# A Mamba and mixture-of-experts layer in one kernel: the four z products in one slot as raw copies, their silu in one group, and three other moves

## The chip, the cores and the metric

The kernel runs on one core of one Trainium2 chip. Its time is the device time of one execution in microseconds; below, "us" is always that. The time of a version is the median of several executions.

## What is computed

Two sequences of 4096 tokens with 256 features go through a layer of two residual branches:

```python
x = x + layernorm(mamba(layernorm(x)))
x = x + layernorm(ffn(layernorm(x)))

# mamba: W_in gives x_in and z (512 channels each)
xz = einsum('bld,de->ble', x, W_in)
x_in, z = split(xz, 2)
u = silu(causal_conv4(x_in) + conv_b)            # 4 taps per channel
dt_lr, Bm, Cm = split(u @ W_xproj)               # 16, 16, 16
delta = softplus(dt_lr @ W_dt + b_dt)
h = exp(delta * A) * h + (delta * u) * B_t       # 16 states per channel, over 4096 steps
y = (sum over states of h * C_t) + D_skip * u
out = (y * silu(z)) @ W_out

# ffn: a shared expert, and the two best of 8 experts by a softmax router
shared = (silu(x @ shared_gate) * (x @ shared_up)) @ shared_down
routed = sum over e of coef[t, e] * ((silu(x @ gate_e) * (x @ up_e)) @ down_e)
```

## The kernel before

**Tiling.** The 8192 tokens are cut into 16 chunks of 512 (`CHUNKS`). The 512 channels are 4 groups of 128 partitions (`J`), the tokens of a chunk 4 blocks of 128 (`NT`). A chunk's scan has 16 states times 4 channel groups: 64 slots (`SLOTS`), one scan instruction (L753, VectorE) in each. Slot t handles state t // 4, group t % 4.

**Stages.** Every engine runs the same loop, `body(s, lo, r)`, for s = -2 to 17. In body s the scan is that of chunk s (`with_scan`), the out-projection, norms and FFN are those of chunk s-1 (`ffn`), and the x and z products, convolution, silu and softplus are those of chunk s+1 (`prep`). The norm of the input of chunk s+2 (tile `xa`) is made too. So bodies 2 to 14 all hold the same work; body 0 has no FFN part, and body 15 no prep part. Body -1 is the prologue, body 16 the FFN of the last chunk with no scans.

**Order of the work.** Each engine's instructions are written out by hand: a table of slot numbers (`XIN_PE`, `SILU`, `Y_POOL` and so on, from L188) says in which of the 64 slots an engine issues a step, and the order of the `if`s in `body` sets the order inside a slot. Engines meet only by semaphores (a `Stage` holds one, `at(chunk, k)` is the count to wait for).

**What happens between slot 60 of one body and slot 14 of the next,** where the change lies:

- ScalarE makes `d_a` (the decay, exp, L602) two slots ahead of the scan: the one for scan t+2 is issued in slot t and waits until scan t has freed one of the two PSUM banks. So the scans and ScalarE are coupled: whatever ScalarE does between two decays must fit beside the VectorE work of the same slots. exp and silu use different function tables; the compiler puts an ACT_TABLE_LOAD before the first of each run. Copies and Identity are issued under either.
- TensorE transposes the states (L445) so that VectorE can add them into `y_t` (L763, two adds in every even slot; state 0 is copied by ScalarE, L610, slots 5 to 8). It also makes the x products (L433, slots 4, 4, 7, 8), which ScalarE and VectorE turn into the convolution `u` (L698, then L907, slots 6, 7, 10, 11), and the z products (L556): groups 0 and 1 in slot 9 into the banks `dn`, groups 2 and 3 in slots 60 and 61 into the banks `ring`. ScalarE takes silu of u 0, 1 and z 0, 1 in slot 8, of u 2, 3 in slot 11, and of z 2, 3 in slot 62.
- The transposes of the normed input (`x_t`, L423) are in slot 0 of body s for chunk s+1, and their copies (L688) in slot 1.
- The out-projection: `y_d` (L770) in slot 3, times silu(z) on GpSimd (`gate_y`, L1033, slot 4, behind that slot's `d_bu`), the products with W_out (L469, slots 5 and 6), then the norm's moments on VectorE (`O_STATS`, slot 8: L774, L780), its rstd on GpSimd (`rstd_of("o")`, L953 to L961), the add to the stream (L786, slot 9), the moments and rstd of x1, the normed x1 (ScalarE, L619), its transposes (TensorE, L490, slot 10) and copies (ScalarE, L660).
- GpSimd makes the inflow `d_bu` (L987) in every even slot, keeps the last column of each state (L1026, every fourth slot), multiplies the FFN's hidden tiles (L1040, L1045), makes the six small operations of the convolution's head (`before_chunk`, L932 to L944) in slot 1, and adds the FFN's result to the stream (`add_stream_y`, L976) in slot 7.
- The moments of the FFN's result (`Y_STATS`, slot 60) stand in VectorE's order between scan 60 and the two adds of slot 60. They wait for the last down products (L536).

## Time and profile before

| | |
|---|---|
| median of 3 runs | 2431.92 us (2430.57 to 2432.0) |
| the profiled execution | 2430.07 us |
| its span, first to last instruction | 2428.1 us |
| granted TensorE clock, mean | 0.938 |
| busiest engine | VectorE, 2228.7 us, 92% of the span |
| VectorE waits for others, whole span | 171 us, of which 47.4 in one wait of the last body |

The profiled execution took 1.85 us less than the median. The span is 1.97 us shorter than that execution's own time. A row of a timeline has the start in us, the duration (for "x2" of the merged pair), engine, line, operation, tiles and shapes; the bracket is how long the engine was idle before it, and what released it. A row of a window has each engine's busy time in that stretch and the clock granted to TensorE (1.00 is 2.4 GHz, 0.50 is 1.2 GHz).

### The profile page before, as it was taken

To read this page: it belongs to the slowest core of one execution; us is meant where nothing else is said; L and a number is where in the kernel's file an instruction comes from. 1 tells how busy PE (TensorE), PEld (TensorE's weight loads), DVE (VectorE), ACT (ScalarE), POOL (GpSimd) and SP (SyncE) were. 2 spreads that over 40 slices of the span, in tenths; PEclk is the share of its full clock that TensorE was granted. 3 is DMA by queue.
4 is the path that set the end of the run, shared out by engine and by line. 5 is a ranking of instruction groups with operands and counts; after the bars stand their busy time and mean duration, and the time that the engine had idled before them with its cause. 6 is when DMAs were issued, how large, how long until landed. Compare 5 with 4: busy or idle time off the path is not lost. (4 is left out here: it accounts for less than half of the span.)

```text
span 2428.1 us, 29696 instructions
## 1 busy us (share of the span) xinstructions
PE 2073.8 (85%) x8960; PEld 1322.8 (54%) x8960; DVE 2228.7 (92%) x3176; ACT 1601.1 (66%) x2358; POOL 1906.6 (79%) x1566
## 2 busy tenths in 40 slices
PE   5668989889898988989888898888989898896977
PEld 2445555656555555655655555555555555564544
DVE  3999999999999999999999999999999999998950
ACT  4556767676776767777677676667677676675632
POOL 3576887969789696978969788796978879698844
PEclk9659999999999999999999899999999999998989
DMA  4111211111121121111211121121112111111101
GB/s 135 34 34 42 70 53 57 58 49 57 53 62 57 49 57 58 57 53 58 65 46 47 58 65 55 55 57 50 56 53 62 61 49 53 49 57 48 65 23 44
DMA packets 92943, 134.23 MB, mean 55 GB/s; under 512 B 12000, under 2 KB 42976, under 8 KB 92784
## 3 DMA queue, kind: packets, MB, share of 16 engines
q1 hardware_dynamic: 92784, 132.34, 18.2%
q8 instruction: 72, 1.18, 0.2%
q14 instruction: 87, 0.71, 0.1%
HBM read 123.13 MB, written 9.18 MB: 54 GB/s over the span
## 5 line engine op out<-in xcount | busy, mean ns | idle before, releaser
L753 DVE TENSOR_TENSOR_SCAN h<-d_a,carry,d_bu 128x512 f32<-128x512 f32 x1024 | 1262.0, 1267 | 35.8 <-ACT d_a L602 35.4
L987 POOL TENSOR_TENSOR d_bu<-delta_u,b_rows 128x1024 f32<-128x1024 f32 x512 | 1202.3, 2357 | 5.1 <-DMA b_rows<-b_rows_hbm 0.9
L602 ACT ACTIVATE d_a<-delta,a_neg 128x512 f32<-128x512 f32 x1024 | 696.4, 689 | 622.2 <-DVE h L753 620.2
L445 PE MATMUL ht<-ident,h 128*128 128x128 f32 x4096 | 618.1, 295 | 116.8 <-DVE y_t L763 111.8
L445 PEld LDWEIGHTS ht<-ident,h 128*128 128x128 f32 x4096 | 503.7, 151 | 367.5 <-issue 132.0
L763 DVE SCALAR_TENSOR_TENSOR y_t<-ht,c_t,y_t 128x512 f32<-128x512 f32 x960 | 665.5, 734 | 2.8 <-PE ht L445 2.6
L509 PE MATMUL ring<-x_t,w_gate_sb 128*128 128x512 f32 x640 | 329.1, 641 | 20.6 <-ACT delta L718 19.1
L516 PE MATMUL ring<-x_t,w_up_sb 128*128 128x512 f32 x640 | 296.4, 606 | 23.0 <-ACT silu_gate L671 22.8
L536 PE MATMUL dn<-w_down_sb,hidden 128*128 128x256 f32 x1280 | 304.3, 381 | 13.2 <-POOL hidden L1045 13.2
L1040 POOL TENSOR_TENSOR hidden<-silu_gate,up 128x512 f32<-128x512 f32 x160 | 204.3, 1277 | 135.8 <-ACT up L675 77.9
L536 PEld LDWEIGHTS dn<-w_down_sb,hidden 128*128 128x128 f32 x1280 | 236.0, 190 | 74.8 <-issue 31.8
L1026 POOL TENSOR_TENSOR carry<-h,one 128x4 f32<-128x4 f32 x256 | 51.2, 200 | 238.7 <-DVE h L753 238.4
L516 PEld LDWEIGHTS ring<-x_t,w_up_sb 128*128 128x128 f32 x640 | 116.6, 191 | 151.7 <-issue 117.0
L602 ACT ACT_TABLE_LOAD x152 | 195.0, 1283 | 2.7
L509 PEld LDWEIGHTS ring<-x_t,w_gate_sb 128*128 128x128 f32 x640 | 121.3, 210 | 121.8 <-issue 90.7
L1045 POOL TENSOR_TENSOR hidden<-hidden,coef_rows 128x512 f32<-128x512 f32 x128 | 162.6, 1271 | 10.0
L907 DVE SCALAR_TENSOR_TENSOR u<-ring,conv_w_sb,u 128x511 f32<-128x511 f32 (+2 forms) x192 | 143.7, 748 | 6.8
L433 PE MATMUL ring<-x_t,w_in_sb 128*128 128x512 f32 x256 | 124.0, 629 | 17.7 <-DVE y_d L770 10.8
L469 PE MATMUL dn<-w_out_sb,y_d 128*128 128x256 f32 x512 | 114.5, 382 | 7.1 <-POOL y_d L1033 7.1
L774 DVE BATCH_NORM_STATS2 stats_o<-dn 128x6 f32<-128x256 f32 x128 | 45.4, 416 | 74.1 <-PE dn L536 65.4
L469 PEld LDWEIGHTS dn<-w_out_sb,y_d 128*128 128x128 f32 x512 | 96.0, 190 | 22.6 <-POOL y_d L1033 10.2
L675 ACT ACTIVATE up<-ring 128x512 f32<-128x512 f32 x160 | 92.8, 580 | 22.4 <-PE ring L516 22.4
(111 smaller groups left out, 1868.7 us busy)
## 6 DMA issues: line engine op xcount, KB each, us to landing
b_rows<-b_rows_hbm SPq DMA_DIRECT2D x256, 256.0 KB, 3.5
coef_rows<-coef_rows_hbm SPq DMA_DIRECT2D x128, 256.0 KB, 3.5
xa<-L_attn_x_in SPq DMA_DIRECT2D x16, 512.0 KB, 5.1
xr<-L_attn_x_in SPq DMA_DIRECT2D x16, 512.0 KB, 5.2
out<-xr SPq DMA_DIRECT2D x16, 512.0 KB, 2.9
w_in_sb<-L_attn_W_in_in SPq DMA_DIRECT2D x1, 1024.0 KB, 6.4
w_gate_sb<-L_ffn_experts_gate_in SPq DMA_DIRECT2D x2, 512.0 KB, 4.5
w_up_sb<-L_ffn_experts_up_in SPq DMA_DIRECT2D x2, 512.0 KB, 5.4
```

The source lines that it names most:

```text
L445: last = nc.tensor.transpose(HT[q % HTS][:, j * P:(j + 1) * P], H[:, (NS * c + n) % HS, j, a * P:(a + 1) * P], IDN[:, :])
L469: last = nc.tensor.matmul(DN[a // 2][:, (a % 2) * DM:(a % 2 + 1) * DM], YD[:, j, a * P:(a + 1) * P], WO[:, j, :], start=(j == 0 and a % 2 ...
L509: last = nc.tensor.matmul(bank[:, :], WG[:, k, f, :], X1T[:, k, :], start=(k == 0), stop=(k == KM - 1))
L516: last = nc.tensor.matmul(bank[:, :], WU[:, k, f, :], X1T[:, k, :], start=(k == 0), stop=(k == KM - 1))
L536: last = nc.tensor.matmul(DN[a // 2][:, (a % 2) * DM:(a % 2 + 1) * DM], HF[:, f % 2, a * P:(a + 1) * P], WD[:, f, :], start=(f == 0 and a ...
L602: nc.scalar.activation(DA[i % DAS][:, :], DL[:, r, j, :], ACT.Exp, scale=ANEG[:, j, n:n + 1]).then_inc(ex.sem, 1)
L753: nc.vector.tensor_tensor_scan(H[:, (NS * s + n) % HS, j, :], DA[(n * J + j) % DAS][:, :], BU[:, (2 * n + j // 2) % 4, j % 2, :], CARRY[:, ...
L763: nc.vector.scalar_tensor_tensor(YT[:, a, :], HT[q % HTS][:, :], CT[:, r, a, n:n + 1], YT[:, a, :], ALU.mult, ALU.add).then_inc(add_c.sem, 1)
L907: nc.vector.scalar_tensor_tensor(U[:, o, j, back:], bank[:, 0:T - back], CW[:, j, k:k + 1], U[:, o, j, back:], ALU.mult, ALU.add)\
L987: nc.gpsimd.tensor_tensor(BU[:, (2 * n + h) % 4, :, :], DU[:, 2 * h:2 * h + 2, :], BB[:, n % 2, :].unsqueeze(1).to_broadcast([P, 2, T]), A ...
L1040: nc.gpsimd.tensor_tensor(HF[:, f % 2, :], TG[:, f % 2, :], UP[:, f % 2, :], ALU.mult).then_inc(hf.sem, 1)
L1045: nc.gpsimd.tensor_tensor(HF[:, f % 2, :], HF[:, f % 2, :], CB[:, e % 2, :], ALU.mult)\
```

## The change

Five things move; all numbers are slots.

1. **z products.** All four (L555 in the new file) are in slot 9, through the two banks `dn` in turn. ScalarE copies each raw into `silu_z` (L713; groups 0 and 1 in its slot 8, 2 and 3 in its slot 9 behind the normed x1), counted by the new semaphore `z_raw`. TensorE waits for copy j-2 before product j, and for all four before it transposes x1 into the same banks. The silu of all four (L719), in place, is one group in slot 60. In the prologue (no chunk to scan) it stands behind the silu of u 2, 3 in slot 11 (`SILU_FIRST`).
2. **x_t.** The transposes of chunk s+2 go to slot 58 of body s, the copies to slot 59, instead of slots 0 and 1 of the next body. The moments of `xa` are spread over slots 26, 32, 36 and 42, closed in slot 46, with the rstd in 47 and the normed `xa` in 50.
3. **Tap groups' silu.** The silu of u 0 and 1 is in slot 7, ahead of state 0's copy of that slot.
4. **GpSimd.** The head of the convolution is in slot 15 of the body before. `gate_y` stands ahead of `d_bu` in slot 4. `add_stream_y` is in slot 8, behind `rstd_of("o")`.
5. **Y_STATS** is still in slot 60, behind that slot's two adds.

```diff
-        Y_POOL = 7
+        Y_POOL = 8
-        XA_STATS, XA_RSTD, XA_NORM = (32, 32, 42, 42), 44, 49
+        XA_STATS, XA_MEAN, XA_RSTD, XA_NORM, XT_PE, XT_ACT = (26, 32, 36, 42), 46, 47, 50, 58, 59
-        Z_PE, Y_STATS = (9, 9, 60, 61), 60
-        SILU = {8: [("u", 0), ("u", 1), ("z", 0), ("z", 1)], 11: [("u", 2), ("u", 3)], 62: [("z", 2), ("z", 3)]}
+        Z_PE, Z_ACT, Y_STATS = 9, (8, 8, 9, 9), 60
+        U_EARLY, HEAD_POOL = 7, 15
+        SILU = {11: [("u", 2), ("u", 3)], 60: [("z", j) for j in range(J)]}
+        SILU_FIRST = {11: SILU[11] + SILU[60]}
...
                 if t == X1T_PE:
                     if exists(lo + 1):
-                        pe.wait_ge(sz.sem, sz.at(s + 1, 2))
+                        pe.wait_ge(z_raw.sem, z_raw.at(s + 1))
...
                         if j < 2:
                             pe.wait_ge(resid["o"].sem, resid["o"].at(s - 1, 2 * j + 2))
                         else:
-                            pe.wait_ge(*ring_user_before(s, lo, "z", j))
+                            pe.wait_ge(z_raw.sem, z_raw.at(c, j - 1))
                         for k in range(KM):
-                            last = nc.tensor.matmul(z_bank(j)[:, :], WIN[:, k, DI + j * P:DI + (j + 1) * P],
+                            last = nc.tensor.matmul(DN[j % 2][:, :], WIN[:, k, DI + j * P:DI + (j + 1) * P],
...
+                    if prep and t == U_EARLY:
+                        for k in range(2):
+                            silu_u(s + 1, o, k)
                     if with_scan and NT < t <= 2 * NT:
                         first_state(s, r, t - NT - 1)
...
+                for j in range(J):
+                    if t == Z_ACT[j]:
+                        act.wait_ge(full["z"].sem, full["z"].at(c, j + 1))
+                        act.wait_ge(y_gate.sem, y_gate.at(s - 1))
+                        nc.scalar.activation(SZ[:, o, j, :], DN[j % 2][:, :], ACT.Copy).then_inc(z_raw.sem, 1)
...
+                        nc.scalar.activation(SZ[:, o, k, :], SZ[:, o, k, :], ACT.Silu).then_inc(sz.sem, 1)
...
-                    if with_scan and n + 1 < NS and t % 2 == 0:
-                        inflow(s, n + 1, t % NT // 2)
-                    if ffn and t == 60:
-                        rstd_of("y", s - 1)
                     if ffn and t == Y_GATE:
                         for j in range(J):
                             gate_y(s - 1, o, j)
+                    if with_scan and n + 1 < NS and t % 2 == 0:
+                        inflow(s, n + 1, t % NT // 2)
...
-                    if prep and t == 1:
-                        before_chunk(s + 1, o)
+                    if exists(lo + 2) and t == HEAD_POOL:
+                        before_chunk(s + 2, r)
```

**ScalarE, slots 7 to 11 of a body with all parts.** Before (L610 is state 0's copy, L694 and L698 the taps of an x product, L704 silu of u, L708 silu of z, L619 the normed x1, L660 the copies of its transposes):

```order
271 L610 ACTIVATE y_t<-ht,c_t 128x512
272 L694 ACTIVATE halo<-ring 128x3
273 L698 ACTIVATE u<-ring,conv_b_sb,conv_w_sb 128x509
274 L694 ACTIVATE halo<-ring 128x3
275 L698 ACTIVATE u<-ring,conv_b_sb,conv_w_sb 128x509
276 L704 ACT_TABLE_LOAD
277 L704 ACTIVATE u<-u 128x512 x2
278 L708 ACTIVATE silu_z<-dn 128x512 x2
279 L602 ACT_TABLE_LOAD
280 L602 ACTIVATE d_a<-delta,a_neg 128x512
281 L619 ACTIVATE up<-xr,mean_rstd_x,rstd_x 128x256 x4
283 L660 ACTIVATE x_t<-dn 128x512 x2
```

And with the change, from the silu of u 0 and 1 on (L694 is now the silu of u, L713 the raw copies, L618 the normed x1, L668 the copies of its transposes):

```order
272 L694 ACT_TABLE_LOAD
273 L694 ACTIVATE u<-u 128x512 x2
274 L609 ACTIVATE y_t<-ht,c_t 128x512
275 L601 ACT_TABLE_LOAD
279 L706 ACTIVATE u<-ring,conv_b_sb,conv_w_sb 128x509
281 L706 ACTIVATE u<-ring,conv_b_sb,conv_w_sb 128x509
282 L713 ACTIVATE silu_z<-dn 128x512 x2
283 L601 ACTIVATE d_a<-delta,a_neg 128x512
284 L618 ACTIVATE up<-xr,mean_rstd_x,rstd_x 128x256 x4
285 L713 ACTIVATE silu_z<-dn 128x512 x2
286 L601 ACTIVATE d_a<-delta,a_neg 128x512
287 L668 ACTIVATE x_t<-dn 128x512 x2
```

The silu group of slot 8 has lost its two z and moved ahead of the taps; two copies stand before the normed x1, and two between it and the copies of its transposes.

**GpSimd, slots 0 to 9 of such a body.** Before:

```order
245 L987 TENSOR_TENSOR d_bu<-delta_u,b_rows 128x1024
246 L932 TENSOR_TENSOR head<-halo,conv_w_sb 128x12
251 L944 TENSOR_TENSOR head<-head,conv_b_sb 128x12
254 L987 TENSOR_TENSOR d_bu<-delta_u,b_rows 128x1024
255 L1033 TENSOR_TENSOR y_d<-y_d,silu_z 128x512 x4
256 L987 TENSOR_TENSOR d_bu<-delta_u,b_rows 128x1024
257 L976 TENSOR_TENSOR xr<-xr,silu_gate 128x1024
258 L1026 TENSOR_TENSOR carry<-h,one 128x4
259 L987 TENSOR_TENSOR d_bu<-delta_u,b_rows 128x1024
260 L953 TENSOR_TENSOR var_eps_o<-mean_var_o,eps 128x4
```

With the change:

```order
243 L998 TENSOR_TENSOR d_bu<-delta_u,b_rows 128x1024 x2
244 L1037 TENSOR_TENSOR carry<-h,one 128x4
245 L1044 TENSOR_TENSOR y_d<-y_d,silu_z 128x512 x4
246 L998 TENSOR_TENSOR d_bu<-delta_u,b_rows 128x1024 x2
247 L1037 TENSOR_TENSOR carry<-h,one 128x4
248 L998 TENSOR_TENSOR d_bu<-delta_u,b_rows 128x1024
249 L964 TENSOR_TENSOR var_eps_o<-mean_var_o,eps 128x4
251 L972 TENSOR_TENSOR mean_rstd_o<-mean_var_o,rstd_o 128x4
252 L987 TENSOR_TENSOR xr<-xr,silu_gate 128x1024
253 L964 TENSOR_TENSOR var_eps_x<-mean_var_x,eps 128x4
```

The head is gone from slot 1, `gate_y` passed one `d_bu`, and `add_stream_y` (the xr row) passed from before `rstd_o` to behind it.

**ScalarE, slots 58 to 63.** Before, the silu of z 2, 3 stands between the decays 0 and 1 of the next chunk, and the copies of x_t behind the next body's decay 3:

```order
251 L602 ACTIVATE d_a<-delta,a_neg 128x512 x7
252 L708 ACT_TABLE_LOAD
253 L708 ACTIVATE silu_z<-ring 128x512 x2
254 L602 ACT_TABLE_LOAD
255 L602 ACTIVATE d_a<-delta,a_neg 128x512 x2
256 L628 ACTIVATE silu_gate<-dn,mean_rstd_y,rstd_y 128x256 x4
257 L602 ACTIVATE d_a<-delta,a_neg 128x512
258 L688 ACTIVATE x_t<-ring 128x512 x2
```

With the change the copies stand before decay 62 and the group of four before decay 63:

```order
254 L601 ACTIVATE d_a<-delta,a_neg 128x512 x4
255 L657 ACTIVATE x_t<-ring 128x512 x2
256 L601 ACTIVATE d_a<-delta,a_neg 128x512
257 L719 ACT_TABLE_LOAD
258 L719 ACTIVATE silu_z<-silu_z 128x512 x4
259 L601 ACT_TABLE_LOAD
260 L601 ACTIVATE d_a<-delta,a_neg 128x512 x4
```

The number of table loads in such a body is the same; the group is two silu longer and two slots earlier.

## Rows read from the trace of the kernel before

**Rows 1.** The page, busy time, share of the span and instructions of each engine

```profile
PE 2073.8 (85%) x8960; PEld 1322.8 (54%) x8960; DVE 2228.7 (92%) x3176; ACT 1601.1 (66%) x2358; POOL 1906.6 (79%) x1566
```

**Rows 2.** The waits of VectorE: us in total, times, longest

```profile
DVE stats_o L774 <- PE dn L536: 65.4, 16, 47.4
DVE h L753 <- ACT d_a L602: 35.4, 78, 12.4
DVE xr L786 <- POOL rstd_o L956: 21.4, 16, 2.5
```

**Rows 3.** The timeline of VectorE, slot 60 to slot 14 of the next body

```profile
746.57 1.42 DVE L774 BATCH_NORM_STATS2 stats_o<-dn 128x6 f32<-128x256 f32 x4 [1.20 <-PE dn L536]
748.33 1.38 DVE L763 SCALAR_TENSOR_TENSOR y_t<-ht,c_t,y_t 128x512 f32<-128x512 f32 x2
...
780.86 1.66 DVE L786 SCALAR_TENSOR_TENSOR xr<-dn,rstd_o,xr 128x256 f32<-128x256 f32 x4 [1.28 <-POOL rstd_o L956]
...
796.86 1.28 DVE L753 TENSOR_TENSOR_SCAN h<-d_a,carry,d_bu 128x512 f32<-128x512 f32 x1 [0.32 <-ACT d_a L602]
```

**Rows 4.** The timeline of GpSimd, slots 1 to 16 of that body

```profile
761.32 0.21 POOL L932 TENSOR_TENSOR head<-halo,conv_w_sb 128x12 f32<-128x12 f32 x1
...
774.69 2.35 POOL L976 TENSOR_TENSOR xr<-xr,silu_gate 128x1024 f32<-128x1024 f32 x1
...
777.16 2.35 POOL L987 TENSOR_TENSOR d_bu<-delta_u,b_rows 128x1024 f32<-128x1024 f32 x1
...
779.74 1.02 POOL L956 TENSOR_TENSOR rstd_o<-var_eps_o,minus_half 128x4 f32<-128x4 f32 x1
...
784.32 0.20 POOL L953 TENSOR_TENSOR var_eps_x<-mean_var_x,eps 128x4 f32<-128x4 f32 x1 [3.28 <-DVE mean_var_x L780]
...
800.71 0.20 POOL L1026 TENSOR_TENSOR carry<-h,one 128x4 f32<-128x4 f32 x1 [5.42 <-DVE h L753]
```

**Rows 5.** The timeline of VectorE, slot 9 of body 1

```profile
204.94 1.66 DVE L786 SCALAR_TENSOR_TENSOR xr<-dn,rstd_o,xr 128x256 f32<-128x256 f32 x4 [0.30 <-POOL rstd_o L956]
```

**Rows 6.** The timeline of TensorE, slots 9 and 10, and slot 59

```profile
744.54 1.99 PE L536 MATMUL dn<-w_down_sb,hidden 128*128 128x256 f32 x8 [0.82 <-POOL hidden L1045]
...
781.79 3.70 PE L556 MATMUL dn<-x_t,w_in_sb 128*128 128x512 f32 x8 [0.66 <-DVE xr L786]
788.79 2.07 PE L490 MATMUL dn<-ident,up 128*128 128x128 f32 x8 [3.31 <-ACT up L619]
```

**Rows 7.** The timeline of ScalarE, slots 9 to 13

```profile
788.07 2.06 ACT L619 ACTIVATE up<-xr,mean_rstd_x,rstd_x 128x256 f32<-128x256 f32 x4
...
790.69 1.08 ACT L660 ACTIVATE x_t<-dn 128x512 f32<-128x512 f32 x2
...
794.83 1.28 ACT L602 ACT_TABLE_LOAD   x1
796.13 1.30 ACT L602 ACTIVATE d_a<-delta,a_neg 128x512 f32<-128x512 f32 x2
```

**Rows 8.** The timeline of GpSimd, slots 44 and 47

```profile
860.99 0.20 POOL L953 TENSOR_TENSOR var_eps_xa<-mean_var_xa,eps 128x4 f32<-128x4 f32 x1
...
865.93 1.28 POOL L1040 TENSOR_TENSOR hidden<-silu_gate,up 128x512 f32<-128x512 f32 x1 [0.80 <-issue]
```

**Rows 9.** The timeline of VectorE, the first scan of body 0

```profile
50.51 1.28 DVE L753 TENSOR_TENSOR_SCAN h<-d_a,carry,d_bu 128x512 f32<-128x512 f32 x1 [12.43 <-ACT d_a L602]
```

**Rows 10.** The timeline of VectorE, slots 8 and 9 of body 15

```profile
2212.18 1.62 DVE L774 BATCH_NORM_STATS2 stats_o<-dn 128x6 f32<-128x256 f32 x4 [2.05 <-PE dn L469]
...
2217.89 1.66 DVE L786 SCALAR_TENSOR_TENSOR xr<-dn,rstd_o,xr 128x256 f32<-128x256 f32 x4 [2.51 <-POOL rstd_o L956]
```

**Rows 11.** Windows: busy us of PE, PEld, DVE, ACT, POOL, then clock, DMA share, GB/s

```profile
140.00:160.00 20.00, 11.98 (x50) 10.05 (x51) 19.97 (x28) 10.57 (x18) 13.46 (x12) 0.50 0.14 39
```

**Rows 12.** The timeline of TensorE, x products 0 and 1 of bodies 0 and 9

```profile
57.98 6.66 PE L433 MATMUL ring<-x_t,w_in_sb 128*128 128x512 f32 x8 [4.38 <-ACT x_t L688]
...
1339.32 4.28 PE L433 MATMUL ring<-x_t,w_in_sb 128*128 128x512 f32 x8
```

57 lines of the change are left out of this document (29 added, 28 removed).

## The prediction

> **What bounds the kernel now.** I read the page first: VectorE is busy for 2228.7 of 2428.1 us [rows 1], so in the steady bodies only VectorE's waits can be won, and 199 us of idle is all there is. Then the waits of VectorE [rows 2]. The 65.4 us on the down products hold one of 47.4 in the last body; the other 15 are 1.20 each. The 21.4 us before L786 are 13 of about 1.3, and three more at both ends. Of the 35.4 us on decays, 17.9 lie in body 0; the rest is about 1.1 per body in pieces. Then the timeline of VectorE over one seam between bodies [rows 3], which I follow slot by slot: from slot 60 to slot 14 it stands still three times, 1.20 us before the moments of y, 1.28 before L786, 0.32 before scan 14. Last, the other engines in the same stretch [rows 4, 6, 7], to see what each wait ends on and what is late next. The order of VectorE hardly changes, so this is a change of what VectorE waits for.
>
> **Moments of y behind the two adds.** The down products end at about 746.5 [rows 6], the moments start at 746.57, 1.20 after scan 60. The two adds take 1.38, less what overlaps the next instruction, 1.30 [rows 3], so they fill the 1.20. Not all of it stays. The rstd of xa (four small operations, 1.8 us of GpSimd from 860.99) moves from slot 44, where GpSimd had 0.80 idle behind it, to slot 47, ahead of the hidden tile of 865.93 [rows 8]. With the moments of xa closed in slot 46 (by the replay of VectorE's scans at about 864.5) it ends at 866.4, so that tile is 0.45 later; 0.15 of that is absorbed on the way, and the down products of slot 59, which wait for GpSimd already [rows 6], come 0.3 later. The moments then wait 0.3 instead of 1.20. The closing of xa's moments in slot 46 fills a 0.2 wait for a decay. **Gain 1.0 per body**, between 0.2 (if the rest of GpSimd's queue passes on more of its 1.8) and 1.4.
>
> **GpSimd before rstd_o.** In slot 8 the moments of o are ready about 1 us before GpSimd comes to them at 779.5, when `d_bu` (2.35 us from 777.16) ends; ahead of that stood `add_stream_y` (2.35 from 774.69) and the six head operations (0.21 each and gaps, 1.34 in all from 761.32) [rows 4]. With both gone from before it (3.7 us, of which the later rstd of xa takes 0.3), GpSimd is free at about 776.2. What the wait is then, body 1 shows, which has no `add_stream_y` yet: 0.30 [rows 5]. **Gain 0.98 per body.** `add_stream_y` behind rstd_o hides beside L786 and the x1 moments: 2.35 against the 3.28 that GpSimd stood idle there. `gate_y` ahead of one `d_bu` makes that `d_bu` ready at 771.4; scan 8, wants it at about 774. The head in slot 15 lies in 5.42 us of idle [rows 4]. All three cost nothing; without that cover each would cost its own length.
>
> **z products in slot 9, the chain to scan 14.** This takes back. Counting from the start of L786 (780.86), before: the first product at 0.93, the second ready at 4.67 [rows 6], silu 0.6, table load 1.28, decay 11 0.69 (two take 1.30), the four normed x1 from 7.2 to 9.2, their transposes behind them from 7.9, the copies from 9.8, decay 13, load, two silu, load, and decay 14 ends at 16.0, which is when scan 14 starts [rows 3, 7]. Now: TensorE runs four products, 7.4 us, from 1.0 to 8.3. ScalarE copies z 0 at 3.0 and z 1 at 4.7, decay 11 follows at 5.3 with no load, the normed x1 run from 5.95 to 7.95, the copies of z 2 and 3 to 9.1. The transposes start at 9.2, and as all four x1 are there, they take about half of the paced 2.07, 1.04. Copies 10.1 to 11.1, decay 13, load 1.28, two silu 1.15, load 1.28, decay 14 at 16.25. VectorE without waits needs 15.7. So scan 14 waits 0.55 instead of 0.32: **cost 0.25 per body**. The bounds: VectorE-bound, a gain of 0.32, and a cost of 2.1 if nothing of the transposes' pacing is won back and the copies queue one behind the other. I take the replay, since each duration in it is a row. The product of slot 9 that sets it off also waits for TensorE itself: x products, states and out-projection in front of it end at 779.7, L786's second result at 779.6. TensorE has next to no slack there.
>
> **ScalarE, slots 58 to 63.** The copies of x_t (1.06 us) and the group of four silu (load 1.28, 2.3, load 1.28) put decay 63 at about 752.0; scan 63 wants it at 752.2. Nothing lost, with 0.2 to 0.3 of cover, which is there because the moments of y stand in slot 60. In body 0 there are none: **1.9 us lost once**. Here a rule is weighed. The row shows a load of 1.28 us and the next activation 1.30 after its start, at 794.83 and 796.13 [rows 7]. The Trainium skill (ScalarE: Activation LUTs, What ACT_TABLE_LOAD costs) gives 1283 ns for the load and another 1380 ns of drain for every switch; by that, decay 63 would be 2.8 later and some 35 us would be lost over the bodies. The load agrees, of the drain the trace shows nothing.
>
> **Silu of u 0, 1 in slot 7** starts when convolution 1 is done, at 774.3, and leaves ScalarE before the x products 2, 3 need it; no VectorE wait hangs on it, between 0 and 0.2 of cost.
>
> **The ends.** Body 15 has no z and no convolution. There L774 waits 2.05 for the out-projection and L786 2.51 for rstd_o [rows 10]; `gate_y` one `d_bu` (2.35) earlier and GpSimd free give back 1.1 and 2.2; with the 1.0 of body 14's moments 4.3, and 1.2 for its own. The prologue pays. Scan 0 waits 12.43 on ScalarE [rows 9]. There z 2, 3 and all four silu now come before `x_dbl` (about 4.2 us), and the copies of x_t, with a wait for TensorE, before decay 0 (2). Against that, the silu group between decays 0 and 1 is gone (3.65), and scans 1 to 6 wait no more: 2.6 late at the first convolution, and 1.7 more by slot 14 of body 0, where no FFN work covers four products: 4.3 in all, between 0 and 7.
>
> **The sum.** Per body 1.0 + 0.98 - 0.25 = 1.73, for the 13 seams before bodies 2 to 14: 22.5. Body 15 4.3 + 1.2. Against: prologue and body 0 4.3, its slot 60 1.9, body 1 0.1. That is 28.0 - 6.3 = 21.7. I take off 2 for the clock, see below: 19.7. The profiled execution took 2430.07, so 2410.4; the median of the runs lies 1.85 above it, so I forecast **2412 us**.
>
> **The rivals.**
> 1. *The low clock reaches the x products.* In body 0, with little but transposes, TensorE is granted 0.50, its lower level of 1.2 GHz [rows 11]. At each seam only transposes now run from the down products to the x products, 16 us instead of 12. Before, 3 of 14 seams entered the x products at the low clock and lost 0.6 (4.28 against 3.67 [rows 12]); that is where my 2 us come from. If half of each group runs low, TensorE is 1 us later at z 0, and so is decay 14: 13 us lost, 2425. The Trainium skill (TensorE: Matmul & The Clock Gate, the entries on transpose mode) says that transposes don't count as activity as matmuls do; body 0's 0.50 agrees.
> 2. *The z chain makes it slower.* The same place, at full price: a whole group at the low clock takes 6.66 instead of 3.67 [rows 12], 3 us later at z 0 with no slack, and 13 times 3 is 39 against the 21.7: 2449. It turns slower from 1.7 us per seam on. For it: no slack on TensorE and one more handshake (TensorE, ScalarE, TensorE) per bank. Against: in the trace the clock came back within the first products, whenever it had fallen.
> 3. *No loss at scan 14.* If the two engines overlap better than I replayed, scan 14 waits for nothing: 0.57 more per body, 7 us: 2403.
> 4. *Nothing is won:* the chain to decay 14 keeps its old end, since every gain before it only lengthens the wait there. Then only body 15's 5.5 is left, against 6.3: 2432.
> 5. *The drain of the skill's rule* shows where the cover is thin: a loss at decay 63 of 2.5 us in 14 bodies, 2445.
>
> **How the numbers follow.** Forecast (2405 to 2419) 0.57; rival 1 0.16; rival 2 0.07; rival 3 0.11; rival 4 0.08; rival 5 0.01. Range 2401 to 2427: it takes in rivals 1 and 3, the bounds of the prologue, and 0.4 us per body to either side. A measurement of this kernel can tell 0.2%, 4.9 us, from no change. Faster 0.85, same 0.07, slower 0.08.
>
> **What would show it.** The wait of the y moments at 0.3 (right) or near 1.2; that before L786 at 0.3; the wait before scan 14 at 0.5 to 0.6, not 2; scan 63 without a wait but in body 0; scan 0 at about 57. Wrong would be: a VectorE wait at scan 14 of over 1.5, x products of over 5 us at most seams, or new waits before scans 2 and 4.

## The result, and the profile after the change

| | before | with the change |
|---|---|---|
| median | 2431.24 us (2429.9 to 2432.0, 4 runs) | 2404.24 us (2401.76 to 2408.07, 4 runs) |
| profiled execution, its span | 2430.07, 2428.1 | 2401.76, 2400.0 |
| granted clock, mean | 0.938 | 0.922 |

The ratio is 0.9891, with a 95% interval of 0.9874 to 0.9908: 1.1% faster. The forecast was 2412, within 2401 to 2427. The profiled execution is the fastest of the four, 2.5 us under their median, so a sum of waits read from its trace and a difference of medians can differ by some us.

In the new file the scan is L764, the decay L601, the adds into `y_t` L774, the moments L785 and L791, the add to the stream L797, the down products L537, the x products L434, the raw z copies L713. The waits of VectorE (us in total, times, longest), which answer to [rows 2]:

```profile
DVE stats_o L785 <- PE dn L537: 52.9, 14, 47.4
DVE h L764 <- ACT d_a L601: 37.2, 43, 17.8
...
DVE xr L797 <- POOL rstd_o L967: 7.9, 16, 1.8
```

Beside the 47.4 of the last body, 5.5 us in 13 waits are left for the down products (18 before), and 7.9 for rstd_o (21.4 before). The decays cost slightly more in total, in 43 waits instead of 78: one of 17.8 is scan 0. Busy time has hardly changed, VectorE's least of all (compare [rows 1]):

```profile
PE 2065.5 (86%) x8960; PEld 1344.7 (56%) x8960; DVE 2225.6 (93%) x3176; ACT 1628.4 (68%) x2420; POOL 1907.1 (79%) x1566
```

The timeline of VectorE over the same seam as [rows 3]:

```profile
744.57 1.42 DVE L785 BATCH_NORM_STATS2 stats_o<-dn 128x6 f32<-128x256 f32 x4 [0.41 <-PE dn L537]
...
776.55 1.66 DVE L797 SCALAR_TENSOR_TENSOR xr<-dn,rstd_o,xr 128x256 f32<-128x256 f32 x4 [0.30 <-POOL rstd_o L967]
...
792.59 1.28 DVE L764 TENSOR_TENSOR_SCAN h<-d_a,carry,d_bu 128x512 f32<-128x512 f32 x1 [0.37 <-ACT d_a L601]
```

The start of L797 (L786 before) is a good mark for timing a body, since it comes once in each. Between bodies 1 and 14 its starts lie 1871.35 us apart before (204.94 to 2076.29) and 1842.05 after (209.39 to 2051.44): 143.95 and 141.70 per seam. I call the mean per seam **the distance** below. The span lost 28.1 us: the 13 seams won 29.3, bodies 14 and 15 won 3.6 more, 4.45 are given back up to body 1, and 0.3 in the epilogue.

Ten of the 13 seams look like the one above. Three have a long wait at scan 14, as here:

```profile
509.98 1.28 DVE L764 TENSOR_TENSOR_SCAN h<-d_a,carry,d_bu 128x512 f32<-128x512 f32 x1 [1.53 <-ACT d_a L601]
```

The timeline of TensorE in that seam shows why. The transposes of `y_t` take 1.97 and 1.91 (1.09 and 1.04 where the clock is back in time), and the x products behind them 4.89 instead of 3.67. From 475.57 on TensorE never stops, so the z products start at 494.97, 2.2 us after L797 instead of 0.9:

```profile
473.81 1.97 PE L459 MATMUL ring<-ident,y_t 128*128 128x128 f32 x8 [1.18 <-DVE y_t L774]
475.57 1.91 PE L459 MATMUL dn<-ident,y_t 128*128 128x128 f32 x8
477.28 4.89 PE L434 MATMUL ring<-x_t,w_in_sb 128*128 128x512 f32 x8
...
494.97 7.03 PE L555 MATMUL dn<-x_t,w_in_sb 128*128 128x512 f32 x16
```

The other seams with slow x products are those whose L797 starts at 1059.59 (4.79, wait 1.43) and 1626.06 (4.87, wait 1.50); 4.00 goes with a wait of 0.63.

### The profile page after: what moved, and what is told of

Same layout as the page of the kernel before. It is cut to its first block and busy times, and to the rows that moved or that the text cites. A ratio compares the mean times of both kernels' runs of the same rounds, so it can differ in the third digit from the quotient of the medians.

```text
span 2400.0 us, 29790 instructions
## 1 busy us (share of the span) xinstructions
PE 2065.5 (86%) x8960; PEld 1344.7 (56%) x8960; DVE 2225.6 (93%) x3176; ACT 1628.4 (68%) x2420; POOL 1907.1 (79%) x1566
## 5 line engine op out<-in xcount | busy, mean ns | idle before, releaser
L764 DVE TENSOR_TENSOR_SCAN h<-d_a,carry,d_bu 128x512 f32<-128x512 f32 x1024 | 1262.0, 1267 | 40.5 <-ACT d_a L601 37.2
L601 ACT ACTIVATE d_a<-delta,a_neg 128x512 f32<-128x512 f32 x1024 | 696.4, 689 | 583.6 <-DVE h L764 581.8
L446 PEld LDWEIGHTS ht<-ident,h 128*128 128x128 f32 x4096 | 517.9, 154 | 376.3 <-DVE y_t L774 156.0
L774 DVE SCALAR_TENSOR_TENSOR y_t<-ht,c_t,y_t 128x512 f32<-128x512 f32 x960 | 665.6, 735 | 1.6 <-PE ht L446 1.2
L510 PE MATMUL ring<-x_t,w_gate_sb 128*128 128x512 f32 x640 | 314.8, 616 | 25.0 <-ACT delta L729 21.0
L537 PE MATMUL dn<-w_down_sb,hidden 128*128 128x256 f32 x1280 | 304.3, 381 | 15.5 <-POOL hidden L1056 15.5
L517 PE MATMUL ring<-x_t,w_up_sb 128*128 128x512 f32 x640 | 298.6, 610 | 21.7 <-ACT silu_gate L679 21.4
L537 PEld LDWEIGHTS dn<-w_down_sb,hidden 128*128 128x128 f32 x1280 | 235.9, 190 | 77.1 <-issue 28.7
L510 PEld LDWEIGHTS ring<-x_t,w_gate_sb 128*128 128x128 f32 x640 | 113.5, 197 | 122.7 <-issue 83.8
L434 PE MATMUL ring<-x_t,w_in_sb 128*128 128x512 f32 x256 | 128.2, 646 | 6.3 <-DVE y_d L781 3.4
L555 PE MATMUL dn<-x_t,w_in_sb 128*128 128x512 f32 x256 | 113.3, 595 | 0.7 <-DVE xr L797 0.7
```

Of the source, the lines that this page charges most:

```text
L446: last = nc.tensor.transpose(HT[q % HTS][:, j * P:(j + 1) * P], H[:, (NS * c + n) % HS, j, a * P:(a + 1) * P], IDN[:, :])
L510: last = nc.tensor.matmul(bank[:, :], WG[:, k, f, :], X1T[:, k, :], start=(k == 0), stop=(k == KM - 1))
L517: last = nc.tensor.matmul(bank[:, :], WU[:, k, f, :], X1T[:, k, :], start=(k == 0), stop=(k == KM - 1))
L537: last = nc.tensor.matmul(DN[a // 2][:, (a % 2) * DM:(a % 2 + 1) * DM], HF[:, f % 2, a * P:(a + 1) * P], WD[:, f, :], start=(f == 0 and a ...
L601: nc.scalar.activation(DA[i % DAS][:, :], DL[:, r, j, :], ACT.Exp, scale=ANEG[:, j, n:n + 1]).then_inc(ex.sem, 1)
L764: nc.vector.tensor_tensor_scan(H[:, (NS * s + n) % HS, j, :], DA[(n * J + j) % DAS][:, :], BU[:, (2 * n + j // 2) % 4, j % 2, :], CARRY[:, ...
```

## The experiments

All times below are medians, and "distance" is the mean over the same 13 seams of the profiled run. Each diff is against the changed kernel unless it says otherwise.

### Moments of y ahead of the adds again

In VectorE's order, the block goes back into `ffn_part`, which stands ahead of the adds:

```diff
+                if t == Y_STATS:
+                    dve.wait_ge(down.sem, down.at(c))
+                    for a in range(NT):
+                        moments("y", c, a, dn(a))
+                    moments_end("y", c)
...
-                    if ffn and t == Y_STATS:
-                        dve.wait_ge(down.sem, down.at(s - 1))
-                        for a in range(NT):
-                            moments("y", s - 1, a, dn(a))
-                        moments_end("y", s - 1)
```

> The changed kernel, with the moments of y put back between scan 60 and the two adds; all else stays. Theory (the prediction's first term): the adds no longer cover the end of the down products, so VectorE waits 0.4 + 1.3 = 1.7 us at L785 instead of 0.42 in the 14 bodies that have these moments, 16 to 18 us in all: 2418 to 2423. Rival: most of what the seams won came from elsewhere (GpSimd, the xa moments), and the wait comes back only at the size of 0.2 to 0.4 per body: 2407 to 2411.

2425.01 us, ratio to before 0.9974 (0.9965 to 0.9983). Distance 143.37.

```profile
750.73 1.43 DVE L785 BATCH_NORM_STATS2 stats_o<-dn 128x6 f32<-128x256 f32 x4 [1.74 <-PE dn L537]
```

The wait is 1.70 to 1.75 in all 13 bodies, as the theory had it. The distance is 1.67 longer, 1.3 of it from this wait; 0.4 to 0.5 in most bodies are waits for transposed states in the middle of the body. Against that, the x products take 3.60 wherever all eight are recorded from body 1 on, and no scan 14 waits over 0.37, which is 0.3 less per seam. So the first term holds at its full size. One line of position is worth 21 us; this wait alone makes 17 in the 13 seams. The time lies 2 us above the theory's range, which did not have the waits for transposed states.

### The moments of xa as before

```diff
-        XA_STATS, XA_MEAN, XA_RSTD, XA_NORM, XT_PE, XT_ACT = (26, 32, 36, 42), 46, 47, 50, 58, 59
+        XA_STATS, XA_MEAN, XA_RSTD, XA_NORM, XT_PE, XT_ACT = (32, 32, 42, 42), 42, 44, 49, 58, 59
```

> The changed kernel, with the moments, rstd and norm of xa in their old slots (32, 32, 42, 42, closed in 42; 44; 49). Theory: the spread moments fill waits of 0.19 for decays, which come back at three places per body (0.6 us), while rstd of xa no longer stands ahead of a hidden tile and the wait before the moments of y falls by about 0.2: net 0.3 to 0.4 in 14 bodies, 4 to 6 us slower, 2408 to 2410. Rival 1: only the later rstd counts, and the kernel is 2 to 4 us faster. Rival 2: nothing, within 1 us.

2405.44 us, ratio 0.9901 (0.9886 to 0.9916), distance 141.64. Rival 2 holds (1.2 us more, with intervals that overlap), and both mechanisms are there. Three waits of 0.19 for decays are back in each body, as before:

```profile
860.81 2.46 DVE L764 TENSOR_TENSOR_SCAN h<-d_a,carry,d_bu 128x512 f32<-128x512 f32 x2 [0.19 <-ACT d_a L601]
...
886.77 1.41 DVE L785 BATCH_NORM_STATS2 stats_o<-dn 128x6 f32<-128x256 f32 x4
```

And the moments of y wait for nothing any more. The first combined version below, where the closing and the rstd of xa go back and the spread stays, has no such wait either, so the whole 0.41 came from them. What comes back (0.57) is made good by this 0.41 and by the long waits at scan 14, which don't occur here (0.50 is the longest; 0.28 less per seam).

### GpSimd's two moves taken back

```diff
-        Y_POOL = 8
+        Y_POOL = 7
...
-                    if exists(lo + 2) and t == HEAD_POOL:
-                        before_chunk(s + 2, r)
+                    if prep and t == 1:
+                        before_chunk(s + 1, o)
```

> The changed kernel, with add_stream_y back in slot 7 and the head of the convolution back in slot 1; gate_y stays ahead of d_bu. Theory (the prediction's second term): rstd_o is late again, the wait before L797 goes from 0.30 to about 1.3 in bodies 2 to 14 and by 1 to 2 in body 15, so 13 to 16 us slower, 2417 to 2420, and the waits at scan 14 stay. Rival: L797 later means that the chain to scan 14 has its time in the wait either way, and half or less of it shows: 2404 to 2410.

2437.73 us, ratio 1.0034 (1.0022 to 1.0047): slower than the kernel before. Distance 144.12. Both sides were wrong: 33 us, twice the theory's figure.

```profile
788.12 1.66 DVE L797 SCALAR_TENSOR_TENSOR xr<-dn,rstd_o,xr 128x256 f32<-128x256 f32 x4 [2.64 <-POOL rstd_o L967]
```

The wait is 2.64, not 1.3. GpSimd's timeline in this run has one stop of 1.00 at 727.48, for the mean of xa, and none over 0.15 from there to rstd_o at 787.00:

```profile
727.48 0.20 POOL L964 TENSOR_TENSOR var_eps_xa<-mean_var_xa,eps 128x4 f32<-128x4 f32 x1 [1.00 <-DVE mean_var_xa L791]
...
781.93 2.38 POOL L987 TENSOR_TENSOR xr<-xr,silu_gate 128x1024 f32<-128x1024 f32 x1
...
787.00 1.02 POOL L967 TENSOR_TENSOR rstd_o<-var_eps_o,minus_half 128x4 f32<-128x4 f32 x1
```

That is 59.5 us in which GpSimd is the bound, and it explains the distance: L797 starts at 642.75, the chain begins 84.73 later, takes 59.52, and L797 follows rstd_o's start by 1.12, together 145.37 for this seam. It is one with a long wait at scan 14 (below); in most of the others the chain begins 83.03 after L797, and 83.03 + 59.52 + 1.12 = 143.67, as they are. Nothing that VectorE wins behind the mean of xa can shorten it; it only waits longer for rstd_o. The chain also begins later than before, when GpSimd had the rstd of xa behind it by slot 44 and stood idle for 0.80 ahead of the hidden tile [rows 8]. In waits, 1.36 more here stand against 0.78 fewer at the moments of y and 0.57 fewer at three decays. So with GpSimd as it was, all other parts together win nothing in a seam. Whether xa in its old slots would have left some of it wasn't tried.

In four bodies (2, 4, 8 and 14, three of them in the distance) scan 14 waits 2.06 instead of 0.36, 0.4 per seam, where the three long waits of the changed kernel made 0.3. There the x products are fast (3.67 at most), but TensorE stands idle for 2.34 to 2.68 before the z products, and these take 8.83 where all are recorded, instead of 7.13; in body 2 the granted clock is 0.85 and 0.72 in the windows from 352 to 360. In the other bodies from 3 on TensorE stands idle there for 1.62 to 2.21, and they take 7.13.

### GpSimd's three moves alone

Against the kernel before:

```diff
-        Y_POOL = 7
+        Y_POOL = 8
...
+                    if ffn and t == Y_GATE:
+                        for j in range(J):
+                            gate_y(s - 1, o, j)
                     if with_scan and n + 1 < NS and t % 2 == 0:
                         inflow(s, n + 1, t % NT // 2)
...
-                    if prep and t == 1:
-                        before_chunk(s + 1, o)
+                    if exists(lo + 2) and t == 15:
+                        before_chunk(s + 2, r)
```

> The kernel before with GpSimd's three moves alone (add_stream_y in slot 8, head in slot 15, gate_y ahead of d_bu). Theory: GpSimd runs without a stop from its last hidden tiles to rstd_o, so its moves and the gains ahead of rstd_o are two limits of one stretch: without GpSimd's moves the others won nothing there, and alone they win only their own wait, 1.28 to 0.30, in 13 seams, and 3 to 4 in body 15: 16 us, 2413 to 2417, with a distance between bodies of about 142.9. Rival: the wait before L786 was fed by all parts together, and GpSimd's moves alone win nearly the 33 us that taking them out cost: 2400 to 2405.

2419.43 us, ratio 0.9953 (0.994 to 0.9967), distance 143.31. The wait for rstd_o is 0.30 and that before the moments of y 1.20, as the theory says, and four seams take 142.75, 0.98 less than most had before; the other nine take 143.4 to 144.0, and in each of these VectorE waits 0.3 to 0.9 for transposed states (L445) in the middle of the body. The gain is 11.5 us, smaller than the 16 expected. Alone, GpSimd's moves win 0.64 per seam; two of them, taken out of the whole, cost 2.42 (the third, `gate_y`, is worth nothing in a seam, see below). The terms don't add, and this is the largest thing that the prediction's form, a sum of parts, did not see.

### z products as before

Against the kernel before: GpSimd's three moves as above, the moments of y behind the adds, and

```diff
-        XA_STATS, XA_RSTD, XA_NORM = (32, 32, 42, 42), 44, 49
+        XA_STATS, XA_MEAN, XA_RSTD, XA_NORM = (26, 32, 36, 42), 46, 47, 50
```

> The kernel before with all parts of the change but the z products, the copies of x_t and the place of the silu of u: z 0, 1 in slot 9 with silu in slot 8, z 2, 3 in slots 60 and 61 with silu in slot 62, x_t in slots 0 and 1; moments of y behind the adds, xa spread, GpSimd's three moves. Theory: the z move itself wins nothing. Its costs go: 4.5 of the prologue, 1.7 at scan 63 of body 0, and three waits of 1.1 at scan 14, while scan 14 waits 0.3 as before; so 6 to 10 us faster than the changed kernel, 2394 to 2398. Rival: the z move holds part of the gain, since copies of x_t and a silu group at the start of a body (between decays 0 and 1, behind decay 3) cost VectorE waits once the wait before the moments of y is gone: 2405 to 2415, with waits at scans 1 to 4 of each body.

2400.3 us, ratio 0.9875 (0.9861 to 0.9888), distance 141.84, L797's counterpart in body 1 at 204.57 instead of 209.39. So 4.8 us of the prologue come back, and the seams lose 0.14 each: scan 14 waits 0.24 to 0.48 everywhere, but two bodies have a wait of 1.84 and 2.04 before the moments of y. That is 2 us short of the theory's 2394 to 2398, and the rival's waits at scans 1 to 4 are not there. The intervals of this kernel and of the changed one overlap; it is 4 us ahead by the medians. The z move, which names the change, wins nothing measurable, and the combined versions below show that it costs.

### z products 2 and 3 beside the last hidden tiles

```diff
-        Z_PE, Z_ACT, Y_STATS = 9, (8, 8, 9, 9), 60
+        Z_PE, Z_ACT, Y_STATS = (9, 9, 55, 56), (8, 8, 57, 57), 60
...
-        RING_USE += [("xt", 2, k, k) for k in range(KM)]
+        RING_USE += [("z", 1, j, j % 2) for j in range(2, J)] + [("xt", 2, k, k) for k in range(KM)]
```

> The changed kernel, with z products 2 and 3 in slots 55 and 56 through the banks ring and their raw copies in slot 57; the silu of all four stays one group in slot 60. Theory: the four products in slot 9 cost the wait at scan 14 where the x products run at the low clock (1.4 to 1.5 in three bodies instead of 0.37); with two products TensorE has 3.6 us of room, so those three waits go, scan 14 waits 0.4 or less everywhere, and the prologue is 1.5 to 3.5 shorter, with scan 0 at about 53 to 54: 2397 to 2401. Rival: the two copies and two products beside the last FFN tiles delay the down products, and the wait before the moments of y grows by more than 0.5 per body: 2408 or more.

2426.7 us, ratio 0.998 (0.9971 to 0.9989), distance 143.19. Scan 14 indeed waits for nothing (under 0.15 in every body), also where the x products are slow (4.74 and 4.83 in bodies 11 and 13). So a long wait at scan 14 takes both, slow x products and four z products behind them. But the two products run back to back ahead of a transposed state, which is late for its add:

```profile
743.69 3.60 PE L558 MATMUL ring<-x_t,w_in_sb 128*128 128x512 f32 x8
747.12 1.04 PE L449 MATMUL ht<-ident,h 128*128 128x128 f32 x8
```
```profile
747.76 1.41 DVE L777 SCALAR_TENSOR_TENSOR y_t<-ht,c_t,y_t 128x512 f32<-128x512 f32 x2 [1.92 <-PE ht L449]
```

1.9 us in each of 14 bodies: the rival's size by another mechanism than it named. Scan 0 comes at 59.37, not 53 to 54. In this kernel the prologue's last copies of z and their silu stand in slot 57, ahead of decay 0.

### z of chunk 0 later in the prologue

```diff
-                    if t == Z_PE:
+                    if t == (Z_PE if exists(lo) else CT_PE + 1):
...
-                    if t == Z_ACT[j]:
+                    if t == (Z_ACT[j] if exists(lo) else XA_NORM + 1):
...
-        SILU_FIRST = {11: SILU[11] + SILU[60]}
+        SILU_FIRST = {11: SILU[11]}
+        Z_LATE = {7: (0, 1), 11: (2, 3)}
```

`Z_LATE` is the silu of chunk 0's z, in those slots of body 0.

> The changed kernel, with the z products of chunk 0 behind c_t in the prologue (slot 49), their raw copies in slot 51, and their silu in body 0 beside the silu of u (slots 7 and 11). Theory: x_dbl in the prologue waits for TensorE's four z products and four silu (from 34.0 to 42.8 on ScalarE), which all go from before it; scan 0 starts at 47 to 50 instead of 56.21, and all that follows is that much earlier, less 1 to 2 for the silu in body 0: 2396 to 2399. Rival: the chain to scan 0 runs over the input of chunk 1 (its norm, transposes and copies before decay 0), which doesn't move: scan 0 later than 53, 2401 or more.

2411.28 us, ratio 0.991 (0.9897 to 0.9924): 7 us above the changed kernel, with scan 0 at 60.56 instead of 56.21. `x_dbl` is copied 2.9 us earlier (39.88 instead of 42.79), and the delta is ready at 47.0. But ScalarE works in order, and the four copies now stand between the norm of xa and decay 0; they wait for TensorE until 56.95. The rival's side holds: the chain runs over what stands ahead of decay 0.

### Matmuls among the transposes

```diff
+        KEEP = (SLOTS - NT - 2, SLOTS - NT, SLOTS - NT + 2)
...
                 pe.wait_ge(*added(before, p))
+                if q in KEEP:
+                    nc.tensor.matmul(HT[q % HTS][:, :], WO[:, 0, 0:P], WIN[:, 0, 0:512], start=True, stop=True)
```

> The changed kernel with three matmuls of 128x512 added, of no use, one each before the transposes that stand in slots 59, 63 and 0, into the bank that these transposes then fill; nothing is left out. Theory: the clock falls because only transposes run from the down products to the x products; with matmuls among them it stays at 1.00 in the windows up to the x products, those take 3.67 or less in every body, no scan 14 waits over 0.7, and the kernel is 2 to 4 us faster than the changed one (2400 to 2402), unless the 0.9 us each makes a transposed state late for its add. Rival: three matmuls change nothing of the clock, and each is 0.9 to 1.8 us more on TensorE: waits of VectorE for transposes (L446), 2408 or more.

2426.16 us, ratio 0.9978 (0.9969 to 0.9987), distance 143.22. Each side is half right. The x products take 3.67 wherever all eight are recorded from body 1 on, and no scan 14 waits over 0.37 (windows: busy us of PE, PEld, DVE, ACT, POOL, then the clock):

```profile
751.00:752.00 1.00, 0.00 (x0) 0.00 (x0) 1.00 (x2) 0.98 (x2) 0.87 (x2) 0.82 0.18 66
752.00:753.00 1.00, 0.00 (x0) 0.00 (x0) 1.00 (x2) 0.99 (x2) 1.00 (x1) 0.50 0.00 0
752.00:756.00 4.00, 2.79 (x7) 1.65 (x8) 3.01 (x4) 2.54 (x4) 3.69 (x8) 0.50 0.00 0
756.00:760.00 4.00, 3.65 (x15) 2.12 (x13) 3.36 (x4) 0.99 (x2) 3.87 (x3) 0.69 0.00 0
760.00:764.00 4.00, 2.71 (x16) 1.94 (x17) 4.00 (x6) 2.25 (x5) 4.00 (x4) 1.00 0.34 89
```

The clock still falls to 0.50, and is back before the x products at 766.4. But the first of the three matmuls starts at 753.22, and TensorE had stood idle for 4.04 us before it: the clock fell while nothing ran (PE 0.00 in the first two windows). So the three matmuls stand behind the fall and could not prevent it, and the theory's "the clock falls because only transposes run" is wrong. The price is two waits for transposes, 1.17 and 0.2 to 0.5, in nearly every body. With the traces above, slow x products are what makes scan 14 wait long in the changed kernel, but they are not to be cured in this way.

### Silu of u 0 and 1 in slot 8

```diff
-        U_EARLY, HEAD_POOL = 7, 15
+        U_EARLY, HEAD_POOL = 8, 15
```

In slot 8 it is issued behind the taps and ahead of the z copies.

> The changed kernel, with the silu of u 0 and 1 in slot 8 behind the taps of x products 2 and 3 and ahead of the raw copies, instead of slot 7. Theory (the prediction costed it between 0 and 0.2 per body): no wait of VectorE hangs on it, 2403 to 2406. Rival: the group of 3.7 us with its two table loads now stands between the z products and their copies, TensorE waits for these with products 2 and 3, and scan 14 waits 1.5 to 2.5 more in each of 14 bodies: 2425 to 2440.

2426.0 us, ratio 0.998 (0.9971 to 0.9988), distance 143.29. The rival holds: scan 14 waits 1.79 to 2.73.

```profile
784.75 1.28 ACT L691 ACT_TABLE_LOAD   x1
786.05 1.15 ACT L691 ACTIVATE u<-u 128x512 f32<-128x512 f32 x2
787.11 0.58 ACT L713 ACTIVATE silu_z<-dn 128x512 f32<-128x512 f32 x1
788.64 0.60 ACT L713 ACTIVATE silu_z<-dn 128x512 f32<-128x512 f32 x1 [0.96 <-PE dn L555]
789.25 1.28 ACT L601 ACT_TABLE_LOAD   x1
```

The first z copy ends 3.7 us after L797's start at 783.97 (3.55 with the change), but the return to exp now stands behind the second copy, so decay 11, the normed x1 and the chain to decay 14 are 1.4 later. The place of this silu wins nothing by itself, and it is what keeps the price of four z products in slot 9 at 0.35 per seam.

### gate_y behind d_bu again

```diff
-                    if ffn and t == Y_GATE:
-                        for j in range(J):
-                            gate_y(s - 1, o, j)
                     if with_scan and n + 1 < NS and t % 2 == 0:
                         inflow(s, n + 1, t % NT // 2)
+                    if ffn and t == Y_GATE:
+                        for j in range(J):
+                            gate_y(s - 1, o, j)
```

> The changed kernel, with gate_y behind d_bu in slot 4 as before. Theory (the prediction costed the move at nothing in the seams): the distances between bodies stay at 141.7; in body 15 the wait of 1.92 at scan 8 goes, and one of about 2 for the out-projection comes back at L785: 2402 to 2406. Rival: the out-projection now ends 2.35 later, the moments of o wait for it in every body, and the kernel is 0.5 to 1 us per body slower: 2410 to 2418.

2406.96 us, ratio 0.9902 (0.9888 to 0.9915), distance 141.77. The seams don't feel it. In body 15 the wait at scan 8 goes, but that for the out-projection is 6.01, not 2:

```profile
2192.50 1.63 DVE L785 BATCH_NORM_STATS2 stats_o<-dn 128x6 f32<-128x256 f32 x4 [6.01 <-PE dn L470]
```

From body 14 to 15 it is 142.09 instead of 139.34: the 6.01 is paid, and 1.92 at scan 8 and 1.55 before L797 (0.30 instead of 1.85) are won back. The medians differ by as much, 2.7 us, but their intervals overlap.

### Two combined versions

The first starts from the changed kernel. `SILU_0` is body 0's own table, `Z_LATE` as above:

```diff
-        XA_STATS, XA_MEAN, XA_RSTD, XA_NORM, XT_PE, XT_ACT = (26, 32, 36, 42), 46, 47, 50, 58, 59
+        XA_STATS, XA_MEAN, XA_RSTD, XA_NORM, XT_PE, XT_ACT = (26, 32, 36, 42), 42, 44, 50, 58, 59
...
+        SILU_FIRST = {11: SILU[11]}
+        SILU_0 = {11: SILU[11], 56: SILU[60][:2], 60: SILU[60][2:]}
+        Z_LATE = {22: (0, 1), 26: (2, 3)}
```

> The changed kernel with xa's moments spread (26, 32, 36, 42) but closed in 42 with the rstd in slot 44 (norm in 50), the silu of z of chunk 0 in slots 22 and 26 of body 0 instead of ahead of x_dbl, and body 0's own z silu split over slots 56 and 60. Theory: the wait before the moments of y (0.42) goes, one decay wait of 0.19 comes back, 2 to 3 us in all; scan 0 starts 2 us earlier, and the 1.7 at scan 63 of body 0 goes: 6 us, 2397 to 2399. Rival: the chain to scan 14 takes the gains of the seams as longer waits, 2401 or more.

The second starts from the kernel with z products as before. `z_out` frees the banks `ring`, `z_late` is counted for chunk 0 alone:

```diff
-        XA_STATS, XA_MEAN, XA_RSTD, XA_NORM = (26, 32, 36, 42), 46, 47, 50
+        XA_STATS, XA_MEAN, XA_RSTD, XA_NORM = (26, 32, 36, 42), 42, 44, 50
...
+                        nc.scalar.activation(SZ[:, o, k, :], z_bank(k)[:, :],
+                                             ACT.Silu if k < 2 or exists(lo) else ACT.Copy)\
+                          .then_inc((sz if k < 2 else z_out).sem, 1)
+                if lo == 0 and t == 22:
+                    for k in range(2, J):
+                        act.wait_ge(z_out.sem, z_out.at(s, k - 1))
+                        nc.scalar.activation(SZ[:, 1 - o, k, :], SZ[:, 1 - o, k, :], ACT.Silu)\
+                          .then_inc(z_late.sem, 1)
```

> The kernel z_as_before (z products 2 and 3 in slots 60 and 61) with xa's moments spread (26, 32, 36, 42), closed in 42, rstd in 44, and z 2, 3 of chunk 0 copied raw in the prologue, with their silu in slot 22 of body 0. Theory: the wait of 0.41 (2.04 and 1.84 in two bodies) before the moments of y goes, one of 0.19 comes back: 3 to 6 us; the group with two table loads between decays 0 and 1 of the prologue (3.1 us before scan 1) goes: 2.5; together 2392 to 2396. Rival: the first convolution of body 0 waits for x_t instead, and the waits of 2 are of the clock and stay: 2397 to 2400.

The first took 2402.73 us (0.9884, 0.987 to 0.9897; distance 141.73), above its theory's 2397 to 2399, as its rival said. The second took **2393.43 us** (0.9846, 0.9832 to 0.9859; distance 141.24), within its theory's range and faster than both kernels. The two have the same slots for xa, GpSimd's moves and the moments of y, and their intervals lie apart: four z products in slot 9, with the places of the x_t copies and of the silu of u that go with them, cost 9 us against two in slot 9 and two in slots 60 and 61. By their traces the spans differ by 11.4: 6.1 ahead of L797 in body 1, 6.4 in the 13 seams (0.49 each), less 1.1 behind them. The waits of VectorE in the second:

```profile
DVE stats_o L782 <- PE dn L537: 47.6, 2, 47.4
DVE h L761 <- ACT d_a L603: 29.2, 55, 12.4
```

Only the wait in the last body and one of 0.2 are left for the down products; a decay wait of 0.19 is back per body. Before scan 1 it waits 1.67 instead of 3.14. In the first version the moments of y don't wait either, but one scan 14 waits 1.36 and four 0.76 to 0.80, which takes that gain back: its rival. The split of body 0's silu took its wait at scan 63 from 1.71 to 0.67. But scan 0 does not come earlier (56.77). Without the silu of z, ScalarE waits 1.80 for the products of `x_dbl` instead:

```profile
38.89 0.60 ACT L715 ACTIVATE silu_z<-dn 128x512 f32<-128x512 f32 x1 [1.12 <-PE dn L557]
39.38 1.14 ACT L696 ACTIVATE u<-u 128x512 f32<-128x512 f32 x2
42.32 0.59 ACT L729 ACTIVATE x_dbl<-ring 80x512 f32<-80x512 f32 x1 [1.80 <-PE ring L564]
```

What the prologue pays for is TensorE's four z products ahead of those of `x_dbl`, not their silu.

## Why the prediction was right, and where not

**The moments of y, gain 1.0 with a wait of 0.3 left.** The mechanism was right: the wait went from 1.20 to 0.41, and with this part alone undone it is 1.74. The earlier closing and rstd of xa take the 0.41 away, so their later place is its cause, as argued; it cost 0.4, not 0.3. (Its own terms, 0.9 from this wait and 0.2 from a decay, add up to 1.1, not 1.0.)

**The spread of xa's moments.** The step "fills a 0.2 wait for a decay" counted one wait; three of the four are filled, 0.57. This is a mis-sized term and most of what the forecast lacked per seam: 0.4 in 13 seams is 5 us. The xa experiment shows the three come back. It also shows that the spread and the later rstd together, 0.57 against 0.41 and the long waits, win nothing measurable.

**GpSimd before rstd_o, gain 0.98.** The size was right to the hundredth (1.28 to 0.30). The reading behind it was not complete. I took it as one term among others; the two experiments show a shared limit, in which this part decides whether the others count: 0.64 per seam alone, 2.42 out of the whole. Two fallen expectations say so. Rival 4's outcome, nothing won in a seam, is seen with this part taken back (2437.7), but by another mechanism: GpSimd's run to rstd_o, and not the chain to decay 14.

**z chain, cost 0.25.** The replay gave 0.55 at scan 14; ten seams have 0.36 to 0.63, three have 1.43 to 1.53, on average 0.67, so the cost is 0.35. The x1 transposes started 8.9 after L797 (replayed: 9.2) and took 1.09 (1.04). The three are rival 1, the low clock in the x products, at the full 1.1 us but in three seams of 13 instead of all: 3.4 us, against the 2 that I took off for it. One of them, 1.53, is over the 1.5 that I had named as a sign of being wrong. What rival 1 gave as the reason, that only transposes run in these 16 us, is not what the traces show. TensorE stands idle for 4.04 us there, since two z products have left slots 60 and 61, and the clock falls in this idle time or up to 1.4 us behind its end (the last section has the rows). Body 0, which I took as agreeing, doesn't decide it: TensorE is busy there for only 11.98 of 20 us [rows 11]. Rivals 2 and 3 didn't come.

**The seam as a whole.** 0.78 + 0.98 + 0.57 - 0.35 = 1.98 of the measured 2.25. Of the rest, 0.1 is in waits for transposed states in the middle of the body (0.73 and 0.89 in bodies 4 and 9 before, next to none after), which I had not read. They appear and vanish between versions, and no experiment isolates them. The other 0.17 stands in no wait that the traces list, and stays open.

**ScalarE at slots 58 to 63.** Right: scan 63 waits only in body 0, 1.71 (1.9 forecast). The row on which the rule of the Trainium skill (ScalarE: Activation LUTs, What ACT_TABLE_LOAD costs) was weighed reads the same with the change: the load starts at 744.01 and the silu at 745.30, 1.29 later. And the load starts 0.01 to 0.03 us after the activation ahead of it has ended, in nearly all of the some 300 loads. The trace contradicts the further 1380 ns of drain per switch. Rival 5 didn't come.

```profile
744.01 1.28 ACT L719 ACT_TABLE_LOAD   x1
745.30 2.19 ACT L719 ACTIVATE silu_z<-silu_z 128x512 f32<-128x512 f32 x4
747.51 1.28 ACT L601 ACT_TABLE_LOAD   x1
748.80 1.30 ACT L601 ACTIVATE d_a<-delta,a_neg 128x512 f32<-128x512 f32 x2
```

**Silu of u in slot 7, 0 to 0.2.** No wait comes from it, so the cost was right. The sentence that no wait hangs on it was wrong: with this silu in slot 8 the kernel is 22 us slower.

**gate_y and the ends.** In the seams the move costs nothing, as said. For bodies 14 and 15 I forecast 4.3 + 1.2 and got 2.3 + 1.3. The step that failed is that the move costs nothing because `d_bu` is ready before scan 8 "wants it at about 774": that is true in a body with convolutions. Body 15 has none, scan 8 comes earlier, and waits 1.92. The other step is the 2.2 given back before rstd_o: that wait went from 2.51 only to 1.85, as GpSimd runs without a stop from 2165 on and comes to rstd_o at 2189.66. The wait for the out-projection gave back all of its 2.05, where 1.1 was forecast.

```profile
2184.75 1.28 DVE L764 TENSOR_TENSOR_SCAN h<-d_a,carry,d_bu 128x512 f32<-128x512 f32 x1 [1.92 <-issue]
...
2190.78 1.66 DVE L797 SCALAR_TENSOR_TENSOR xr<-dn,rstd_o,xr 128x256 f32<-128x256 f32 x4 [1.85 <-POOL rstd_o L967]
```

**The prologue.** 4.45 given back up to body 1, against 6.3 (4.3, 1.9 and 0.1). Scan 0 came at 56.21 (57 forecast). The first convolution was 1.8 later, not 2.6, and `x_dbl` 3.0, not 4.2: four silu of z were counted on ScalarE, where TensorE's products are the longer chain (without these silu, in the first combined version, `x_dbl` comes only 0.5 earlier).

In sum the span fell by 28.1 where 19.7 were forecast. The seams gave 6.8 more (0.52 in 13) and the 2 set aside for the clock, which are in their measured distance already; the prologue gave 1.85 more, bodies 14 and 15 gave 1.9 less, the epilogue 0.3 less.

## What to carry to other kernels

Before adding up gains, look for an engine that runs without a stop through the stretch in which they lie: gains of others ahead of its end only lengthen the wait on it, and the part that shortens it looks small alone and decides everything in company. Read a seam's conditions again for the bodies that lack a part (no convolutions, no FFN), since a transfer or tile with slack in the steady body has none there. List the waits of 0.2 too: 0.19 at three places in 14 bodies is 8 us, as long as the cure doesn't cost as much elsewhere. And when work is moved off an engine that is not the bottleneck, ask what fills its place: here, where two z products went, TensorE is idle for 4 us, and its clock is low in what follows.
